# Count fill of a graph kernel: compare constants in PSUM, a ring of three two-bank units, packed register words, six kept pairs of sixteen

## What is computed

```python
dst = jnp.minimum((6250 * jax.random.uniform(k, (200000,)) ** 2.0).astype(jnp.int32), 49999)
...
e = jax.nn.leaky_relu(el[src] + er[dst], NEG_SLOPE)          # layer 1, attention
ex = jnp.exp(e - emax[dst])
alpha = ex / denom[dst]
rst = jax.ops.segment_sum(feat[src] * alpha[..., None], dst, num_segments=N)
...
msg = h[row] * norm[:, None]                                 # layer 3, twice
jax.ops.segment_sum(msg, col, num_segments=n) + b
```

## Time and profile before

| | us |
|---|---|
| median of 3 runs (5595.01 to 5600.52) | 5596.46 |
| the profiled execution | 5595.18 |
| its span in the trace | 5593.3 |
| count fill, first compare to last product | 276.7 to 1291.8 |
| walk, first to last gather that waits for it | 1310.1 to 2520.3 |

### The profile page before, as it was taken

How to read it: one execution, slowest core, us unless ns; L and a number is a source line. 1 busy time by engine, 2 the same in 40 slices (tenths; PEclk the granted TensorE clock), 3 DMA queues, 4 the chain that set the end, 5 groups by cost and what they waited for, 6 DMA issues and landing times. The chain is left out here.

```text
span 5593.3 us, 113294 instructions
## 1 busy us (share of the span) xinstructions
PE 4423.2 (79%) x23328; PEld 3487.0 (62%) x23329; DVE 3263.4 (58%) x10456; ACT 2962.9 (53%) x7576; POOL 2195.7 (39%) x2057
## 2 busy tenths in 40 slices
PE   2566665556888888884799699998999962899997
PEld 1443332224666666663799577776777752799996
DVE  7699776667989998897445533335333355222222
ACT  0325666666777777776233356665566655233332
POOL 2477777776777777772222000000000006122221
PEclk9799877768999999995899899999999975899998
DMA  4368888888777777784566366773444444566665
GB/s 135 108 204 262 273 275 288 288 287 247 230 227 230 229 229 227 228 233 119 168 179 182 85 193 216 219 222 101 126 133 133 134 148 143 167 182 179 181 183 163
DMA packets 623736, 1084.57 MB, mean 194 GB/s; under 512 B 74390, under 2 KB 502093, under 8 KB 616748
## 3 DMA queue, kind: packets, MB, share of 16 engines
q1 hardware_dynamic: 504252, 733.75, 42.7%
q0 software_dynamic: 112144, 268.88, 18.0%
q10 hardware_dynamic: 7200, 80.28, 3.6%
HBM read 782.21 MB, written 309.57 MB: 195 GB/s over the span
## 5 line engine op out<-in xcount | busy, mean ns | idle before, releaser
L713 POOL DMA_INDIRECT arena<-table,arena x1664 | 1713.9, 1030 | 570.6 <-issue 454.1
L1380 PE MATMUL banks<-parts,a_wide 128*128 128x512 f32 x4900 | 1179.3, 399 | 18.7 <-ACT a_wide L1403 18.7
L1380 PEld LDWEIGHTS banks<-parts,a_wide 128*128 128x128 f32 x4900 | 917.9, 189 | 263.5 <-ACT a_wide L1403 47.9
L913 PE MATMUL banks<-arena 128*128 128x261 f32 x3328 | 998.8, 428 | 0.0
L659 PE MATMUL banks<-arena 128*128 128x392 bf16 x2368 | 609.1, 411 | 407.8 <-ACT banks L687 227.7
L1403 ACT CAST a_wide<-arena 128x896 fp32r<-128x896 f16 x700 | 659.0, 942 | 422.2 <-PE banks L1380 406.5
L2321 ACT ACTIVATE rings<-banks,b_sb 128x128 f32<-128x128 f32 x1296 | 370.5, 368 | 828.8 <-PE banks L2354 828.8
L2138 POOL DMA_INDIRECT expert_in<-arena,slot x147 | 161.0, 1095 | 1649.5 <-DVEq L2083 1607.7
L659 PEld LDWEIGHTS banks<-arena 128*128 128x128 bf16 x2368 | 339.2, 150 | 677.2 <-issue 636.4
L913 PEld LDWEIGHTS banks<-arena 128*128 128x128 f32 x3328 | 609.2, 204 | 60.5
L2217 POOL DMA_INDIRECT x_kept<-rings,idx_ring x162 | 251.3, 1551 | 979.8 <-DMA x_kept<-rings,idx_ring 860.3
(11 more groups left out here) (357 smaller groups left out, 5227.9 us busy)
## 6 DMA issues: line engine op xcount, KB each, us to landing
arena<-counts SPq DMA_DIRECT2D x700, 224.0 KB, 2.5
arena<-in_L_ffn_W SPq DMA_DIRECT2D x114, 1024.0 KB, 5.1
edge_rows<-arena SPq DMA_DIRECT2D x364, 264.0 KB, 3.3
arena<-edge_rows SPq DMA_DIRECT2D x364, 264.0 KB
counts<-arena ACTq DMA_DIRECT2D x50, 1568.0 KB, 6.5
arena<-in_L_ffn_w SPq DMA_DIRECT2D x64, 1024.0 KB, 5.1
arena<-near_rows SPq DMA_DIRECT2D x416, 128.0 KB
expert_in<-rings SPq DMA_DIRECT2D x25, 2028.0 KB
```

The costliest lines, as they stand in the source:

```text
L713: pool.indirect_dma_start(out=got[:, r, j, :], out_offset=None, in_=table0, in_offset=bass.IndirectOffsetOnAxis(ap=src_sb[:, 2 * pair + j: ...
L913: last = pe.matmul(banks_a[u][:, 0:mw], onehot[:, u % GS, j, :], msg[:, u % RB, j, 0:mw], start=False, stop=False, skip_group_check=True)
L1380: last = pe.matmul(psum[u][:, 0:2 * D], a_wide[:, at:at + P], parts[:, a * 2 * D:(a + 1) * 2 * D], start=(a == 0), stop=(a == NT - 1))
```

## The change

- The two compare constants are copied once into PSUM banks 6 and 7 (signal `fixed`), and the compares read them from there.
- That leaves six banks: units of two windows instead of four (`UW` = 2, 400 units instead of 200) in a ring of three (`UR` = 3).
- One register word holds the banks of a group of four products, three bits each, over the count of zeroed units in nine bits. PE loads 4 words per 16 products instead of 16, and takes each bank out of the word by a division and a mask. ACT's counts are packed two to a word.
- A bank is now the window modulo 6, which costs other one-row operations when the table is made.
- Six of 16 pairs are kept instead of seven: 312 instead of 364 pairs are gathered during the fill, and 520 instead of 468 during the walk.

```diff
-KEPT = (0, 2, 5, 7, 9, 12, 14)
+KEPT = (0, 3, 6, 8, 11, 14)
...
-UW = 4
+UW = 2
...
-UR = 8 // UW
+UB = 6
+UR = UB // UW
...
-                    link(dve.tensor_copy(ptab, trow[:, 0:BP]))
-                    link(dve.tensor_scalar(ztab, ptab.rearrange("p (g u) -> p u g", u=PG)[:, PG - 1, :],
-                                           UW.bit_length() - 1, None, ALU.arith_shift_right))
+                    link(dve.tensor_copy(ztab, trow[:, 0:BP].rearrange("p (g u) -> p u g", u=PG)[:, PG - 1, :]))
+                    link(dve.tensor_scalar(ztab, ztab, UW.bit_length() - 1, None, ALU.arith_shift_right))
                     link(dve.tensor_scalar(ztab, ztab, 1, None, ALU.add))
-                    link(dve.tensor_scalar(ptab, ptab, 7, 9, ALU.bitwise_and, ALU.logical_shift_left))
-                    lead = ptab.rearrange("p (g u) -> p u g", u=PG)[:, 0, :]
-                    link(dve.tensor_tensor(lead, lead, ztab, ALU.add))
+                    link(dve.tensor_scalar(round_, trow[:, 0:BP], float(4096 // UB + 1), None, ALU.mult))
+                    link(dve.tensor_scalar(round_, round_, 12, None, ALU.arith_shift_right))
+                    link(dve.scalar_tensor_tensor(out=bank_f, in0=round_, scalar=-float(UB), in1=trow[:, 0:BP],
+                                                  op0=ALU.mult, op1=ALU.add))
+                    of_four = bank_f.rearrange("p (g u) -> p u g", u=PG)
+                    link(dve.scalar_tensor_tensor(out=word_f, in0=of_four[:, 3, :], scalar=8.0, in1=of_four[:, 2, :],
+                                                  op0=ALU.mult, op1=ALU.add))
+                    for u in (1, 0):
+                        link(dve.scalar_tensor_tensor(out=word_f, in0=word_f, scalar=8.0, in1=of_four[:, u, :],
+                                                      op0=ALU.mult, op1=ALU.add))
+                    link(dve.scalar_tensor_tensor(out=ptab, in0=word_f, scalar=512.0, in1=ztab,
+                                                  op0=ALU.mult, op1=ALU.add))
...
+                    of_two = etab.rearrange("p (n k) -> p k n", k=2)
+                    link(dve.scalar_tensor_tensor(out=etwo, in0=of_two[:, 1, :], scalar=1024.0, in1=of_two[:, 0, :],
+                                                  op0=ALU.mult, op1=ALU.add))
...
+                        dve.tensor_copy(psum[UB + 1][:, 0:LB * P // 2],
+                                        lanes16.rearrange("p n u -> p (n u)").bitcast(F32)).then_inc(fixed, 1)
+                        dve.tensor_copy(psum[UB][:, 0:KB * KEYS // 2],
+                                        keys16.rearrange("p n u -> p (n u)").bitcast(F32)).then_inc(fixed, 1)
+                        dve.wait_ge(fixed, 2)
...
-                                dve.tensor_tensor(oh_b[:, p // LB % (OR // LB), :, :], lanes16,
+                                dve.tensor_tensor(oh_b[:, p // LB % (OR // LB), :, :], lanes_by,
...
-                                last = dve.tensor_tensor(oh_k[:, p // KB % (OR // KB), :, :], keys16,
+                                last = dve.tensor_tensor(oh_k[:, p // KB % (OR // KB), :, :], keys_by,
...
-                            if p % 16 == 0:
-                                at_ = load_many(mybir.EngineType.PE, ptab, p, 16, 0, 7 * 512 + UNITS,
...
+                            if p % (4 * PG) == 0:
+                                words = load_many(mybir.EngineType.PE, ptab, p // PG, 4, 0, (1 << 21) - 1,
...
+                                bank = pe.snap((word // (1 << (3 * (p % PG)))) & (7 * 512))
...
-                                ends = load_many(mybir.EngineType.Activation, etab, u, UNITS_PER_TILE, 1, BP // PG)
+                                pairs_ = load_many(mybir.EngineType.Activation, etwo, u // 2, UNITS_PER_TILE // 2, 1,
+                                                   (1 << 20) - 1, "two counts of 1 to BP // PG in ten bits each")
```

More of the change, by code:

```diff
@@ L102 @@
 assert NVB * VB == NBP * EB and NVB <= P
[L103 removed]
+assert KEYS <= 512 and BP % OR == 0 and UB % UW == 0 and PG <= UB - UW and UNITS < 512
 assert NG * TB == NT
@@ L378, in count_plan, with aside_row @@
             kiota = tmp(KEYS)
-            assert at[0] <= NT * AW
+            assert at[0] <= (NT + 1) * AW, at[0] - (NT + 1) * AW
             at[0] = (NT + 1) * AW + 4 * PCOL
             onehot_at = at[0]
+            rooms = [onehot_at]
+            def aside_row(width):
+                rooms[0] += width
+                return arena[0:1, rooms[0] - width:rooms[0]]
+            ztab, etab, round_ = (aside_row(n).bitcast(I32) for n in (BP // PG, UNITS, BP))
+            bank_f, word_f = (aside_row(n) for n in (BP, BP // PG))
+            assert all((w * (4096 // UB + 1)) >> 12 == w // UB for w in range(NW))
             onehot16 = onehot.rearrange("p u j n -> p (u j n)").bitcast(BF16).rearrange(
@@ L607, in cook_pe @@
                                      ident[:, :]).then_inc(pe_, 1)
-                hot, done, copied, zeroed = (sem("fill_" + n) for n in ("hot", "done", "copied", "zeroed"))
+                hot, done, copied, zeroed, fixed = (sem("fill_" + n) for n in ("hot", "done", "copied", "zeroed", "fixed"))
+                keys_fixed = psum[UB][:, 0:KB * KEYS // 2].bitcast(F16)
+                lanes_fixed = psum[UB + 1][:, 0:LB * P // 2].bitcast(F16)
+                keys_by = keys_fixed.rearrange("p (n u) -> p n u", u=KB)
+                lanes_by = lanes_fixed.rearrange("p (n u) -> p n u", u=LB)
                 clear = sem("clear")
@@ L645, in fill_pe @@
                         for p in range(BP):
[L646 to L649 removed]
+                            if p % (4 * PG) == 0:
+                                words = load_many(mybir.EngineType.PE, ptab, p // PG, 4, 0, (1 << 21) - 1,
+                                                  "four banks of three bits over a count of 1 to UNITS in nine bits")
+                            word = words[p // PG % 4]
                             if p % PG == 0:
[L651 to L653 removed]
+                                pe.wait_ge(zeroed, pe.snap(word & 511))
                                 if p % LB == 0:
                                     pe.wait_ge(hot, p // LB + 1)
+                                bank = pe.snap(word & (7 * 512))
                             else:
[L657 to L658 removed]
+                                bank = pe.snap((word // (1 << (3 * (p % PG)))) & (7 * 512))
                             last = pe.matmul(psum_all[:, bass.ds(bank, KEYS)], oh_b[:, p // LB % (OR // LB), :, p % LB],
```

16 lines of the change are left out of this document (5 added, 11 removed).

## The result

The change makes the kernel slower: 5632.91 us median (4 runs, 5630.53 to 5637.48) against 5598.49 for the kernel before in the same session (5595.01 to 5601.94). The ratio is 1.0063 with a 95% interval of 1.0047 to 1.0079, a loss of 0.6% that is clear of the noise. I had forecast 5566 and a gain.

A forecast was written before the change was run, and what follows sets the result against it. DVE, then a copy-zeroing-product line, bound the fill, and POOL's gathers the walk; −129 (fill) + 1 (copies) + 93 (walk) + 5 (table) = −30, so 5566 us, range 5490 to 5650.

The forecast's parts named there:

- The bound of the fill before: Count fill: DVE's compares early, 0.314 us per product; late, copy, zeroing and four products in line, 4.6 us per unit.
- the 1154th: Count fill: predicted crossover at window 257; DVE paces the first 1154 products, ACT the other 543 windows.
- Units of two windows: Count fill on ACT: copy or zeroing of 784 columns 813 ns, 1.72 us per unit, 0.86 per window.
- Ring of three, 846 + 40 us: Count fill: 379 us at DVE's pace plus 467 at ACT's, plus 40 for register loads and PE's slow clock: 886.
- Packed words, "I take nothing": PE in the fill: shorter loads against added register operations, ±0.8 us per load, taken as zero.
- PSUM constants: DVE's compares in the fill: reading constants from PSUM keeps the price of 0.314 us per product.
- Kept gathers: POOL during the fill: they just fit, ending near 1040 us if single-SBUF-input compares avoid contention; otherwise binding a fill below 860.
- The walk: Stage after the fill: POOL's gathers bind at 1.255 us each; six kept pairs make it 1303 us, a loss of 93.
- The table: First block, on DVE: the piece of 5.25 us becomes 10.1, a loss of 5 us (3 to 7).
- The rival at one element a cycle: DVE's compares in the fill slow down with PSUM inputs, L634 taking 973 ns: 6075 us in all; chance 10%.
- PE at half clock: Rival: PE at 1.2 GHz bounds the fill at 956 us, giving 5636 us in all; chance 14%.
- The range of the sum: Whole kernel: the change's total of −30 us was given a range of −82 to +10, 5514 to 5606 us.

The follow-up runs named there:

- e1_kept7: The kernel after with seven kept pairs of 16 instead of six: 5536.67 us, ratio 0.9894 to the kernel before.
- e6_pack_only: The kernel before with only the packed register words (four banks per word, ACT's counts packed): 5624.22 us, ratio 1.0043.
- f1_mask6: The kernel after with the mask put ahead of the shift when a bank is taken from its word, six kept pairs: 5541.83 us, ratio 0.9900.
- e2_words16: The kernel after with one register word per product again (16 loaded per 16 products), six kept pairs: 5606.28 us, ratio 1.0016.
- e7_kept8: The kernel after with eight kept pairs of 16 instead of six: 5598.55 us, ratio 0.9996.
- e3_both: The kernel after with one register word per product again and seven kept pairs: 5526.26 us, ratio 0.9878.

## Why the prediction was wrong, point by point

**The bound of the fill before.** Right for both parts: DVE early, and the line of copy, zeroing and group late. The ring of three units broke that line: the products behind the 1154th take 512 us in e1_kept7 where e6_pack_only, with the layout of before, takes 596.

**Units of two windows.** 784 columns were to take 813 ns; they take 810 and 817, and the copies of the kernel after start 1.6 to 1.8 us apart late in the fill (forecast 1.72).

```profile
1099.30 0.81 ACT L713 CAST arena<-banks 128x784 f16<-128x784 f32 x1
...
1100.91 0.81 ACT L713 CAST arena<-banks 128x784 f16<-128x784 f32 x1
...
1102.61 0.81 ACT L713 CAST arena<-banks 128x784 f16<-128x784 f32 x1
```

**Ring of three, 846 + 40 us.** With the register term repaired the fill takes 866 us (f1_mask6), 874 and 879 (two banks in a word). So 886 could be reached, by other words than those of this change. In f1_mask6 the first 1154 products take 392 us (forecast 379) and the rest 473 (forecast 467): of the 40 us that I added, some 20 were used.

**Packed words, "I take nothing". This is the step that failed.** I gave the exchange ends of ±0.8 us per 16 products. For its cost I counted the operations' own 32 ns each, 0.77 us. The trace of after shows 0.33 us between products against 0.162, so 16 products cost 16 x 0.17 = 2.7 us more on PE, three and a half times as much. For its gain I had 0.8 at best, and the load gave 1.1 (1.55 to 0.46). The mistake behind the number was to treat PE as having room since it was 64% busy. What I should have asked is how far it was from being the bound: 8 products x 0.33 = 2.6 us, plus the gap at a load, against DVE's 2.51 us. It takes only 0.31 us per product to make PE the bound. The cost falls early, where DVE had been the bound, and the gain late, where long loads hold PE up: 30 us lost and 18 won against one word per product (e2_words16).

The net of these is 12 us of fill (27 us of time by the medians), not the 69 that I missed. So the nothing was not far off as a difference; it was wrong for both of its parts, and so was the 40 us for "a register load". With 16 loaded words the fill takes 940 us and with four packed ones 952, and 886 needs both prices low at once. f1_mask6 shows that: with one register operation fewer ahead of each product but the first of a group, the fill takes 866 us.

**PSUM constants.** Right: 556 ns against 557, 692 against 688. The rival at one element a cycle (973 ns) is refuted, and with it, for two-byte inputs in this operation, the tier table of the Trainium skill, "VectorE: DVE Perf Modes", section "The perf-mode tier table"; the conditions of "Vector Engine (DVE) Microarchitecture Reference", section "Performance modes", are borne out: two-byte types, unit steps and more than one element in the innermost dimension, which these compares have.

**Kept gathers.** The rule that I named but did not lean on was right: 1.25 us each, done at 1062 us (I had 1040 by it). It changed no term for six kept pairs, but it was the news of this kernel: with gathers that quick, seven kept pairs fit ahead of the walk, and the 93 us that I booked as the price of the change were not needed. I took the number six as given and did not ask what the quicker gathers made of it.

**The walk.** 1299 us for a forecast of 1303. My account of the walk before was half right. POOL's rate, 1165 us for 928 gathers, is close below the 1210 that it takes, but e7_kept8 shows that the pairs' other work sets it: 1199 us with 832 gathers left for the walk, and 1203 with 936. So seven kept pairs lie close to the meeting point of the two limits, and the 45 us of waits that I expected "mostly to go" were there because of the 1.45 us per pair, which a walk paced by POOL hides.

**The table.** The work of DVE behind the table starts 7.6 us later, for a forecast of 5: the operations that read every fourth element take 1.19 us for 592 results, against 0.76 where all inputs are contiguous. I had 0.7 for both. The copies took 1.2 us together (forecast 1.3), and some 1 us more lies ahead of the first compare.

**The rivals.** The outcome, 5633, lies beside "PE at half clock" (5636), with nearly its fill (955 for 956), and for another cause: PE became the bound early, but at a granted clock of 0.93, and at 0.97 to 0.98 the same matmuls follow each other at 0.162 us (e2_words16, e3_both). A number that fits is no evidence for its mechanism.

**The range of the sum.** The ends that I gave the single terms add up to −88 and +86 us. The range of −82 to +10 beside the sum does not follow from them. The measured gain of the fill, 60 us, lies within its own ends (55 to 175), so the terms allowed what came and the sum's range did not.

**What stays open.** Why one register operation of 32 to 36 ns widens the spacing by 0.07 to 0.10 us: the profile books the time as "issue". In f1_mask6 a part may be the address operation, which is longer there (76 ns for 37). The long loads of words go with the gathers and their DMA traffic. After and e1_kept7 differ in the kept pairs alone, and from 1100 to 1230 us the first issues no gather (DMA share 0.27) and the second issues 71 (0.77). The loads there, first of after, then of e1_kept7:

```profile
L646 PEldq TENSOR_LOAD <-arena x19: 328/334/944, 1103.8 to 1225.6; - x19
```

```profile
L646 PEldq TENSOR_LOAD <-arena x19: 328/830/1236, 1102.5 to 1227.4; - x19
```

The median is 0.33 us without gathers and 0.83 with them. Whether the traffic or POOL's own work makes them long is not shown.

## What to carry to other kernels

Before operations are put between the instructions of a fast series, compare the spacing they would make with the pace of the next slower engine, not with that engine's busy share. Where an edit makes a shared resource quicker, look again at every number that was tuned to its old speed: here one constant was worth 69 to 96 us.
